# Gram lower triangle: the first five input tiles loaded as 120 and 8 partitions

## The reference

```python
def reference(inputs):                       # (2048, 64, 256) float32
    Z = jnp.einsum('bnd,bmd->bnm', inputs, inputs)
    li, lj = jnp.tril_indices(64, k=-1)
    return Z[:, li, lj]                      # (2048, 2016)
```

## Time and profile before

| what | value |
|---|---|
| median of three runs | 417.86 us (416.99 to 419.29) |
| the profiled execution: its own time | 417.85 us |
| its span, first to last instruction | 416.1 us |
| so, around the span | 1.75 us |
| PE busy | 377.6 us, 91% |
| DVE busy | 364.5 us, 88% |
| POOL and ACT busy | 199.9 and 178.8 us |
| DMA, load queue and store queue | 135.26 and 15.48 MB |
| one tile's load, issue to landing, median | 17.3 us |

### The profile page before, as it was taken

The page is one execution under the profiler, slowest core; times in us unless marked ns, Lnnn a source line. Parts: engine busy times, 40 slices in busy tenths (PEclk is TensorE's granted clock), DMA queues, the critical chain, the costliest instruction groups (busy, mean ns, idle before and its releaser), DMA issues.

```text
span 416.1 us, 68691 instructions
## 1 busy us (share of the span) xinstructions
PE 377.6 (91%) x33024; PEld 370.4 (89%) x33024; DVE 364.5 (88%) x224; ACT 178.8 (43%) x829; POOL 199.9 (48%) x981
## 2 busy tenths in 40 slices
PE   4469999999999999999999999999999899899940
PEld 4469999999999999999999999999999899898940
DVE  3438899999999999999999998999979799797964
ACT  0011134434555434554345543455544445444465
POOL 1000084664818283564828183563808356182783
PEclk9559999999999999999999999999999999999985
DMA  8259999999999999999999999999999999995218
GB/s 325 87 181 425 426 419 425 418 423 421 420 421 423 423 421 421 422 420 423 380 423 399 388 419 411 403 380 415 347 425 338 422 382 358 392 326 247 68 50 199
DMA packets 21178, 151.01 MB, mean 363 GB/s; under 512 B 2592, under 2 KB 2720, under 8 KB 4768
## 3 DMA queue, kind: packets, MB, share of 16 engines
q1 hardware_dynamic: 18752, 135.26, 81.3%
q10 hardware_dynamic: 2400, 15.48, 9.9%
HBM read 134.22 MB, written 16.52 MB: 362 GB/s over the span
## 4 chain that ended last, share of the span: by engine, by line
PE 55%; DMA 31%; DVE 5%; issue 5%; ACT 2%; ACTq 0%; DVEq 0%
PE bank_set L252 55%; DMA x_in<-x_dram 31%; DVE x_turned L198 4%; ACT packed_rows L120 1%; DVE row_halves L215 1%; ACT packed_rows L126 1%; DVE x_turned L221 0%; ACTq L137 0%; ACT products L279 0%; DVEq L197 0%; ACTq L68 0%; DVEq L214 0%; ACTq L294 0%; ACTq L270 0%
## 5 line engine op out<-in xcount | busy, mean ns | idle before, releaser
L252 PE MATMUL bank_set<-x_turned 32*64 32x64 f32 x33024 | 377.6, 236 | 22.7 <-issue 11.9
L252 PEld LDWEIGHTS bank_set<-x_turned 32*64 32x64 f32 x33024 | 370.4, 132 | 29.8 <-issue 22.6
L198 DVE STREAM_TRANSPOSE x_turned<-x_in 128x2048 f32<-128x2048 f32 x128 | 292.0, 2290 | 41.2 <-PE bank_set L252 18.0
L131 POOL COPY packed_rows<-row_halves 32x60 f32<-32x60 f32 (+30 forms) x961 | 196.4, 206 | 209.2 <-DVE row_halves L215 171.6
L279 ACT COPY products<-bank_set 128x512 f32<-128x512 f32 (+1 forms) x91 | 68.6, 760 | 208.6 <-PE bank_set L252 189.3
L215 DVE STREAM_TRANSPOSE row_halves<-products 128x1024 f32<-128x1024 f32 x64 | 77.1, 1207 | 3.2 <-ACT products L279 2.7
L120 ACT COPY packed_rows<-row_halves 128x32 f32<-128x32 f32 (+30 forms) x481 | 62.8, 220 | 0.0
L126 ACT COPY packed_rows<-row_halves 128x128 f32<-128x128 f32 x256 | 56.9, 300 | 4.3 <-issue 3.0
L279 ACT ACT_TABLE_LOAD x1 | 1.3, 1283 | 19.9 <-PE bank_set L252 19.9
L131 DVE COPY packed_rows<-row_halves 32x2 f32<-32x2 f32 (+30 forms) x31 | 3.4, 187 | 0.0
L120 POOL COPY packed_rows<-row_halves 128x2 f32<-128x2 f32 (+14 forms) x15 | 2.3, 210 | 0.1
## 6 DMA issues: line engine op xcount, KB each, us to landing
x_in<-x_dram SPq DMA_DIRECT2D x128, 1024.0 KB, 17.3
y_dram<-packed_rows ACTq DMA_DIRECT2D x30, 504.0 KB, 8.1
y_dram<-packed_rows SPq DMA_DIRECT2D x2, 380.0 KB, 3.9
y_dram<-packed_rows SPq DMA_DIRECT2D x2, 124.0 KB, 3.6
```

Of the source, the lines that this page charges most:

```text
L131: return copy(packed_rows[first:first + BLOCK, group % 2, :, at + BLOCK:at + i], row_halves[first + BLOCK:first + HALF, i, :, 0:i - BLOCK])
L198: nc.vector.transpose(x_turned[:, j].rearrange("p c b s (h u n v) -> p u v (c b s h) n", h=ROWS // BLOCK, u=PAIRS, v=PAIR), x_in[:, k]).th ...
L252: done = nc.tensor.matmul(bank_sets[s][side * HALF:(side + 1) * HALF, g, at, :].rearrange("r (n u v) -> r u n v", u=PAIRS, v=PAIR), rows, ...
```

## The change

The first five tiles are loaded by two DMAs each: one for partitions 0 to 119, one for partitions 120 to 127. Both count the same semaphore up by 16, so DVE's wait for the five buffers that these tiles use asks for 16 more, in every lap. All other tiles are loaded as before, and so are the order and the waits of SP.

```diff
+    SPLIT_TILES, AHEAD = 5, 120
...
-                sync.dma_start(x_in[:, k], x_joined[t * PARTS:(t + 1) * PARTS]).then_inc(loaded[k], 16)
+                first = t * PARTS
+                if t < SPLIT_TILES:
+                    sync.dma_start(x_in[0:AHEAD, k], x_joined[first:first + AHEAD]).then_inc(loaded[k], 16)
+                    sync.dma_start(x_in[AHEAD:PARTS, k], x_joined[first + AHEAD:first + PARTS]).then_inc(loaded[k], 16)
+                else:
+                    sync.dma_start(x_in[:, k], x_joined[first:first + PARTS]).then_inc(loaded[k], 16)
...
-                dve.wait_ge(loaded[k], (t // IN_RING + 1) * 16)
+                dve.wait_ge(loaded[k], (t // IN_RING + (2 if k < SPLIT_TILES else 1)) * 16)
```

## The result

The changed kernel takes 427.16 us (426.19 to 427.89, five runs) against 417.66 us (416.99 to 419.29, five runs) for the kernel before: ratio 1.0231, 95% interval 1.0208 to 1.0254. It is 9.5 us slower. The forecast was 414.2 us, in a range of 413.0 to 418.8.

A forecast was written before the change was run, and what follows sets the result against it. The prediction took PE's laps and one lagging DMA engine, both hanging on the start, to bound the kernel. Two code fetches gaining 1.85 + 1.75 = 3.6 us, all else nothing, took 417.85 to 414.2 us, range 413.0 to 418.8.

The forecast's parts named there:

- What bounds the kernel: Whole kernel: PE's laps and the lagging engine's work both hang on the start; 3.6 us saved there stays saved.
- both late stages: After the start: PE's gapless laps from 26.5 us, then from 241 to 388 us the chain through loads.
- Code fetches wait behind loads: In the start: loads delay two of PE's code fetches by 1.6 to 2.1 us each; removing this gains 3.6 us.
- The bound of five or six packets in the queue: In the start: a code packet queues behind five or six load packets of 0.31 us, 1.6 to 1.9 us.
- "A packet is one partition's 8192 bytes": First tiles' loads: nine packets of 0.31 us instead of eight; tile 0 lands 0.3 us later, costing at most that.
- Tile 4 "costs none": Last step of the start: tile 4's load needs some 5.1 us and delays neither code fetch nor PE; nothing.
- "Is the empty engine the one that carries the code?": First five tiles: one engine carries all code, and the split leaves that engine without loads; 7 in 10.
- the engine that lags to the end: Late loads: one DMA engine, taken to be the code's, still has its share of the last two tiles to bring.
- The wrong engine is emptied: Rival, chance 0.22: the code's engine keeps its loads, both fetches wait as before; 417.9 us, up to 418.5.
- The delay is the memory's: Rival, chance 0.09: fetches are slow because fifteen engines still read at full rate; 416 to 417.9 us.
- The slower rival: Rival, chance 0.07: the 120 partitions go over eight engines or fewer, tiles take 5.0 us; 421.5 us.
- The five extra DMAs on SP: Issue of the first five tiles: five more DMAs of 0.4 to 0.7 us each on SP; cost nothing.

The follow-up runs named there:

- late4: The kernel before with tile 5 no longer held back until tile 1 is multiplied; 417.35 against 417.60 us.
- nolate: The kernel before with no tile held back, so tiles 4 to 7 follow the first four at once; 421.94 against 417.65 us.
- paced2: The kernel before with the loads of tiles 2 to 5 paced by PE's progress, each shortly after a code packet is asked for; 412.98 against 417.87 us.
- middle64: The kernel before with the first five tiles loaded as partitions 32 to 95, 0 to 31 and 96 to 127; 422.54 against 417.87 us.
- halves64: The changed kernel with its first five tiles split into 64 + 64 partitions instead of 120 + 8; 426.33 against 417.28 us for the kernel before.
- altrows: The changed kernel with the large DMA of the first five tiles reading every second DRAM row, writing the same partitions; 424.35 us, one run.
- only4: The changed kernel with tile 4 alone split into 120 + 8, all others whole; 420.15 against 417.65 us for the kernel before.
- engines8: The kernel before with tiles 1 to 3 each loaded as sixteen DMAs of eight partitions, over eight engines; 423.90 us, one run.
- columns: The kernel before with the first five tiles as two DMAs each of all 128 partitions and half the columns; 418.49 against 417.28 us.
- split112: The changed kernel with its first five tiles split into 112 + 16 partitions instead of 120 + 8; 424.25 against 417.28 us for the kernel before.
- engines7: The kernel before with tiles 1 to 3 each loaded as DMAs of 119, 7 and 2 partitions; 422.12 us, one run.

## Why the prediction was wrong

**What bounds the kernel** held. The early delay goes through both late stages nearly one to one: 8.8 us at the fifth block, 8.2 us in the last lap, 8.3 us between the two profiled executions (426.19 and 417.85 us), 9.5 us between the medians. Slack of 4 us for PE alone was not in the prediction. It is why letting loads go earlier (late4, nolate) gained nothing: the code then came too late.

**Code fetches wait behind loads** held, and it priced the loss. With packets twice as long the two first fetches waited 9.78 - 3.45 = 6.3 us and 18.69 - 12.43 = 6.3 us instead of 3.2. paced2 shows the other side: with the first two tiles landed and no other in flight the second step was 2.2 us shorter, where the prediction had given 1.75 for that fetch. The bound of five or six packets in the queue was wrong; with more loads queued the wait grew to 5.1 us (late4).

**"A packet is one partition's 8192 bytes", eight or nine of them at 0.31 us a tile**: this is the step that failed. The 0.31 us was read from loads of 128 partitions and carried over to one of 120. It measured 0.60 us, so a tile took over 5 us where 2.8 was forecast. By the starts of DVE's turns, tile 0 landed 3.1 us late instead of 0.3, tile 1 5.6 us late instead of 1.0 early. What the runs bear out, for loads of 64 partitions, is that a packet's time hangs on the partitions that are written. The same 64 partitions' worth of load takes 0.31 us a packet at partitions 32 to 95 (middle64) and 0.64 at 0 to 63 (halves64, in the same microsecond). Other rows of DRAM change nothing (altrows, one run of the 120 + 8 split: 0.58 us against 0.59). The DMA views agree: 426 GB/s at 32 to 95, 180 GB/s at 0 to 63, 215 GB/s over both halves from 8 to 12 us. Why the one is fast and the other slow isn't shown, as no record names an engine's partitions. Nor is it for 120 partitions: of the 427 load packets of 8 KB that start in 3 to 20 us the shortest took 0.38 us, so all 15 engines are slow, and that and its cost are what is measured.

**Tile 4 "costs none"** failed for the same reason. It was priced at 5.1 us and took 7.8 (26.40 to 34.19 us); the last code packet queued behind it, 2.46 us late. only4 shows it alone, 2.5 us.

**"Is the empty engine the one that carries the code?"** was put at 7 in 10 and is no: 14.2 load packets beside a code packet, not 15. The premise was wrong too. There is no single code engine: in engines8 the code packet at 21.14 us runs with all eight loading engines still at work, after two that each took the place of a load. Even a correct guess could have helped only some of the fetches. No run shows which engine a load of 120 partitions leaves empty, or that the code's engine stands at an end of their row, so the 7 in 10 stays the author's judgement; what the runs show is that the code came on loaded engines and on one without loads. Whether the engine that lags to the end is the first two packets' engine stays open.

**The rivals.** "The wrong engine is emptied" was true as a fact, with 417.9 us as its price, because it too kept 0.31 us. "The delay is the memory's" falls: code arrives in 1.1 to 1.7 us beside seven or eight loading engines, and beside all 16 too, where their queues are nearly through. In paced2 a fetch asked for at 16.89 us has its packet at 18.01, 1.1 us later, with 16 load packets in flight until 17.75. The kernel before had such a fetch as well, the one asked for at 22.52 us that took 1.6: 15 to 16 load packets were in flight until 24.0 us, which the prediction called "nearly through". The slower rival had the right sign, and tiles of 5 us, for the wrong reason. Fifteen engines were used, and its 421.5 us left out the first two fetches, since it too took each packet at 0.31 us. None of the rivals was that the packets themselves get longer, though their price came from another shape of DMA. That difference of shape was the reason to name such a rival and give it a chance.

**The five extra DMAs on SP** were put at nothing and cost 1.2 us at most: columns has ten DMAs for these tiles as well and lost 1.2 us, of which 0.56 us was in the fifth block already. Its packets of 4 KB move 376 GB/s from 8 to 12 us.

## What to carry to other kernels

A DMA's time per packet belongs to its shape: before a load of all 128 partitions is cut by partitions, measure what a packet of the new shape takes (here 0.31 us whole, 0.60 with 120 + 8). If it must be cut, cut it by columns (1.2 us here instead of 9.5). Of the two cuts of 64 partitions tried, only the one at 32 to 95 kept 0.31 us a packet, and middle64 still lost 4.7 us, as its outer quarters took 0.55. When a kernel's first pass through its code overlaps with full DMA queues, missing blocks of code can wait behind the loads (6.3 us in the changed kernel, 1.1 us in paced2 with none in flight); issue loads just behind a fetch, not just before it (paced2 took 412.98 us against 417.87). A gain in the start counts only if every late chain begins there: here loads and matmuls each had to be moved.

## What the runs showed of the hardware

- Slow packets can get faster while the same kind of load goes on. In engines8 each DMA of tiles 1 to 3 has eight neighbouring partitions, and some eight load packets are in flight (8.0 just before the first two code packets). The packets that start in 5 to 8 us take 0.69 us on average, those in 16 to 20 us 0.46. In the changed kernel they stay near 0.6 us: 0.59 in 8 to 12, 0.62 in 16 to 20. The cause isn't shown.
- Seven packets an engine instead of four or eight (split112, 15.9 load packets in flight) give a mix, 0.40 to 0.78 us from the 10th to the 90th percentile in 8 to 12 us.
- Code packets of 16 KB come on more than one DMA engine (engines7, engines8), and the wait for one grew from 1.1 us on an engine without loads to 6.3 us on one with slow loads queued.
